# Order of the opening in an adaLN transformer kernel: third sequence's layer-norm aggregation, relu of q, and the turning of the gate columns

## The reference

```python
mod = (_silu(L0_c) @ L0_wmod).reshape(L0_c.shape[0], 6, 1, -1)
sa, ca, ga, sb, cb, gb = (mod[:, 0], mod[:, 1], mod[:, 2], mod[:, 3], mod[:, 4], mod[:, 5])
ga = (2 * (ga >= 0) - 1) * jnp.maximum(jnp.abs(ga), 0.25)      # gb alike
h = _layernorm(x, axis=-1) * (1 + ca) + sa
x = x + ga * attn_block(h)
h = _layernorm(x, axis=-1) * (1 + cb) + sb
x = x + gb * channel_mix(h)
```

## Time and profile before

| | |
|---|---|
| time, median of 3 runs | 160.79 us (160.75 to 161.41) |
| the profiled execution | 160.8 us |
| its span from first to last instruction | 159.1 us |
| granted TensorE clock | 0.999 |
| PE, PEld busy | 97%, 89% of the span |
| DVE, ACT, POOL busy | 83%, 80%, 65% |

### The profile page before, as it was taken

How to read it: one execution, slowest core, us unless ns; L and a number is a source line. 1 busy time by engine, 2 the same in 40 slices (tenths; PEclk the granted TensorE clock), 3 DMA queues, 4 the chain that set the end, 5 groups by cost and what they waited for, 6 DMA issues and landing times.

```text
span 159.1 us, 4075 instructions
## 1 busy us (share of the span) xinstructions
PE 153.6 (97%) x1127; PEld 142.4 (89%) x1127; DVE 132.2 (83%) x581; ACT 127.8 (80%) x347; POOL 104.0 (65%) x243
## 2 busy tenths in 40 slices
PE   7998999999999999999999999999999999999992
PEld 7776898989999898999999999989998999888892
DVE  3666888898998989898989899898989797887852
ACT  4455674999898989999898989898998989666562
POOL 4427667594949495867859494949587655962731
PEclk9999999999999999999999999999999999999999
DMA  4938079950010101010010101010100000010102
GB/s 127 280 116 194 12 218 339 417 220 0 2 33 4 33 0 33 6 35 0 0 37 2 33 2 37 0 35 0 37 2 24 13 29 4 0 37 4 33 15 86
DMA packets 9000, 9.95 MB, mean 63 GB/s; under 512 B 737, under 2 KB 7442, under 8 KB 8978
## 3 DMA queue, kind: packets, MB, share of 16 engines
q1 hardware_dynamic: 8656, 9.60, 19.0%
q10 hardware_dynamic: 322, 0.09, 0.2%
HBM read 7.56 MB, written 2.13 MB: 61 GB/s over the span
## 4 chain that ended last, share of the span: by engine, by line
PE 82%; DVE 5%; POOL 4%; issue 3%; ACT 2%; DMA 2%; DVEq 0%; POOLq 0%; ACTq 0%
PE bank L1161 16%; PE bank L1276 15%; PE bank L1150 8%; PE bank L1199 5%; PE bank L1232 5%; PE bank L1248 4%; PE bank L1155 4%; PE bank L1187 4%; PE bank L1240 4%; PE bank L1403 3%; PE bank L1215 3%; PE bank L1211 3%; PE bank L1259 2%; DMA x_all<-in_x 2%; POOL rstd_n L559 1%
## 5 line engine op out<-in xcount | busy, mean ns | idle before, releaser
L1276 PE MATMUL bank<-x1T,w 128*128 128x256 f32 x120 | 30.9, 381 | 0.0
L1161 PE MATMUL bank<-w,hid 128*128 128x128 f32 x240 | 30.0, 275 | 0.0
L1161 PEld LDWEIGHTS bank<-w,hid 128*128 128x128 f32 x240 | 28.5, 192 | 0.0
L559 POOL TENSOR_TENSOR rstd_n<-vare_n,power 128x2 f32<-128x2 f32 x30 | 23.5, 784 | 2.3
L552 POOL TENSOR_TENSOR vare_n<-mv_n,eps 128x2 f32<-128x2 f32 x30 | 6.1, 202 | 28.8 <-DVE mv_n L718 28.7
L354 ACT ACTIVATE hid<-bank,b_cols 128x256 f32<-128x256 f32 x60 | 23.6, 480 | 1.1 <-PE bank L1276 1.1
L1276 PEld LDWEIGHTS bank<-x1T,w 128*128 128x128 f32 x120 | 21.5, 190 | 2.5 <-ACT x1T L332 0.3
L725 DVE TENSOR_SCALAR ny<-bank,mv_ny,rstd_ny 128x128 f32<-128x128 f32 x32 | 11.7, 406 | 4.4 <-POOL rstd_ny L559 4.2
L332 ACT ACTIVATE x1T<-bank,beta_b,cols 128x256 f32<-128x256 f32 x15 | 8.5, 563 | 7.7 <-PE bank L1150 7.6
L835 DVE SCALAR_TENSOR_TENSOR mixT<-bank,modT,keepT 128x256 f32<-128x256 f32 x26 | 12.3, 475 | 1.2
L321 ACT ACTIVATE keepT<-bank,modT 128x255 f32<-128x255 f32 x26 | 13.1, 556 | 0.0
(11 more groups left out here) (183 smaller groups left out, 447.5 us busy)
## 6 DMA issues: line engine op xcount, KB each, us to landing
gm_rows<-mod_rows_dram SPq DMA_DIRECT2D x2, 960.0 KB, 10.6
out<-out_sb SPq DMA_DIRECT2D x15, 128.0 KB, 1.8
gm_rows<-mod_rows_dram SPq DMA_DIRECT2D x1, 768.0 KB, 7.1
w<-in_w SPq DMA_DIRECT2D x1, 512.0 KB, 5.4
x_all<-in_x SPq DMA_DIRECT2D x1, 512.0 KB, 5.7
bv_row<-bv_rows_dram SPq DMA_DIRECT2D x1, 512.0 KB, 7.7
bv_row<-bv_rows_dram SPq DMA_DIRECT2D x1, 384.0 KB, 4.5
gm_rows<-mod_rows_dram SPq DMA_DIRECT2D x1, 384.0 KB, 3.8
```

The costliest lines, as they stand in the source:

```text
L559: nc.gpsimd.tensor_tensor(dest[:, :], vare[name][:, :], power[:, :], ALU.pow).then_inc(rstd_ok[name], 1)
L1161: last = nc.tensor.matmul(banks[6][:, c * D:(c + 1) * D], hid[:, f, c * 128:(c + 1) * 128], w2[:, f, :], start=False, stop=(f == FF - 1 an ...
L1276: return nc.tensor.matmul(bank[:, f % 2 * L:(f % 2 + 1) * L], w1[:, f * 128:(f + 1) * 128], x1T[:, :], start=True, stop=True)
```

## The change

Four reorderings; no instruction is added or removed.

1. DVE: `x_stats(2)` stands ahead of `masked_state(0)` and `x_mv(2)` right behind it (they stood behind it, and behind `attention(0)`). On POOL `first_scale(2)` stands ahead of `gate_parts()`.
2. ACT: `q_relu()` of sequence 1 stands ahead of `state_out(1)`; that of sequence 2 stands behind `attention_turned(1)`, `x1_turned(0)` and `k_exponent(2)`.
3. PE: `attention_product(1)` stands ahead of `turn_gates()`.
4. DVE: at t = 3 `shift_of_n3(0)` stands ahead of `x_stats(5)`, `x_mv(5)` and `masked_state(3)`.

```diff
@@ ACT, first_steps
                 attention_turned(0)
+                q_relu()
                 state_out(1)
-                q_relu()
                 weights_of(2)
...
                 q_exponent(2)
-                q_relu()
                 attention_turned(1)
                 x1_turned(0)
                 k_exponent(2)
+                q_relu()
@@ POOL, first_steps
                 first_scale(1)
+                first_scale(2)
                 gate_parts()
-                first_scale(2)
                 gate_columns()
@@ DVE, first_steps
                 q_elu(0)
+                x_stats(2)
                 dve.wait_ge(const_pool, 9)
                 masked_state(0)
-
-                x_stats(2)
+                x_mv(2)
+
                 denominators(0)
                 reciprocals(0)
                 k_biased(1)
                 attention(0)
-                x_mv(2)
                 k_elu(1)
@@ DVE, step
                     norm_mv("ny", sb_ + 1)
+                    if t == 3:
+                        shift_of_n3(sp_)
                     if live(t + 2):
                         x_stats(t + 2)
                         x_mv(t + 2)
                     masked_state(sa)
-                    shift_of_n3(sp_)
+                    if t > 3:
+                        shift_of_n3(sp_)
                     y_norm(sb_)
@@ PE, first_steps
                 n1_transposes(2)
+                attention_product(1)
                 turn_gates()
-                attention_product(1)
```

## The result

| | before | after |
|---|---|---|
| time, median | 160.81 us (22 runs) | 160.34 us (22 runs) |
| ratio to before | | 0.9968, 95% interval 0.9959 to 0.9977 |
| span of the profiled execution | 159.1 us | 158.5 us |

The ratio is a gain of 0.51 us (0.37 to 0.66). The forecast was 160.55 us, a gain of 0.25 us: the time lies inside its range of 160.0 to 161.05 us, but the gain is about twice the forecast one.

A forecast was written before the change was run, and what follows sets the result against it. The prediction took TensorE, without gaps behind 16 us, to bound the kernel. From 160.8 us it took 0.28 for the opening, added 0.08 for GpSimd holding k_elu(1) and took 0.05 for the n3 shift: 160.55 us, range 160.0 to 161.05.

The forecast's parts named there:

- What bounds the kernel: Behind 16 us a row of TensorE matmuls without gaps; gains only where TensorE stands still, ahead of 16 us and in small waits.
- Part 1, aggregation: DVE and POOL, sequence 2: earlier aggregation lets n1's transposes begin near 15.18 us on TensorE, 0.65 us sooner.
- the rival (c): DVE's x_stats(2): x part 2 not landed in time, kernel slower, 161.05 us with a landing 0.5 us beyond 10.1; chance 0.04.
- Part 2: ACT's relu of q: sequence 1 brings kvs(1) to 15.45 from 16.03 us; sequence 2 taken as 0, at most 0.1 us.
- Part 3: TensorE's order: 0.4 us new wait ahead of attention_product(1); k_product(2) at 16.70 instead of 16.98 us, 0.28 of 0.65 us gained.
- Port: DVE's k_elu(1), held by GpSimd's earlier work: a loss of 0.08 us, bounds 0 and 0.28 us.
- the rival behind the term: At k_elu(1): GpSimd holds it for the full 0.28 us, leaving 160.75 to 160.8 us; chance 0.22.
- The sum: Whole kernel: 160.8 - 0.28 + 0.08 - 0.05 = 160.55 us, chance 0.58.
- Part 4: DVE's shift of n3 at t = 3: 0.05 us gained, bounds -0.1 and 0.17, most given back at state_product(4).

The follow-up runs named there:

- relu2_back: The changed kernel with relu of q of sequence 2 back ahead of attention_turned(1); ratio to before 0.9965 (0.9953 to 0.9977).
- pool_long: The changed kernel with an added SBUF-reading GpSimd sum between first_scale(2) and gate_parts; one run, attention_product(5) 39.63 us behind value_of_state(0) in its trace.
- gates_first: The changed kernel with turn_gates back ahead of attention_product(1); ratio to before 0.9958 (0.9946 to 0.9971).

## Why the prediction was right, and where it was off

- What bounds the kernel: right. Of the 0.51 us gained at the first hidden product 0.46 us are left at `attention_product(5)`. But a gain on the way isn't one at the end: the 0.09 us of the relu of sequence 2 are not among them.
- Part 1, aggregation: right in its times on DVE and TensorE. `x_stats(2)` fits in the idling ahead of `masked_state(0)`, whose place didn't move; the aggregation was forecast for 10.82 us and stands at 10.83 with the offset of 0.08, n1 for 13.85 and stands at 13.85, n1's transposes for 15.18 and stand at 15.18; the rival (c) didn't occur. The gate columns were forecast for 14.8 us and are there at 15.13, and nothing waits for them.
- Part 2: relu of sequence 1 as forecast (q_elu at 14.4 us, 0.11 us of gain through kvs). Relu of sequence 2 costed at nothing: right at the end, by relu2_back.
- Part 3: right in kind. The new wait for kvs(1) stands where it was put, at 0.35 us instead of 0.4 us. `attention_product(1)` starts at 15.75 us on the scale of before, where 15.82 was forecast, and its four instructions (two float32 matmuls) take 0.59 instead of 0.55 us: together 0.03 us better. Hence 0.31 us at `k_product(2)` where the sum had 0.28. That is in part luck: the 0.55 us was read from 16.43 to 16.98 us as the group's own pace, but it holds some 0.06 us of waiting for hT (the same group takes 0.49 us from 24.81 us on), and the group took 0.59 us because it now stands behind a wait.
- Port: **mis-sized**. The term of 0.08 us for GpSimd holding `k_elu(1)` was 0: it took 0.42 us. A gate operation was on hand (0.26 us from 12.95 us on), but ended 0.05 us behind `k_elu(1)`'s start. So `k_elu(1)` came first, and it was POOL's next operation that took longer, 0.48 instead of 0.33 us; the same happened beside `q_elu(1)` (line 594, 0.52 instead of 0.27 us), and with these 0.40 us the gate columns are late. Which of the two would come first was not worked out beforehand, and the margin was small: that the term came to nothing was luck. pool_long shows that the rival behind the term was right as a mechanism, with 0.33 us for an operation of 1.04 us, and my bound of 0.28 us was too low for an operation of that length. POOL after, and at the end the same operation before:

```profile
12.95 0.26 POOL L584 TENSOR_TENSOR gate_size<-gate_sign,raw_mod 128x32 f32<-128x32 f32 x1
13.30 0.48 POOL L586 TENSOR_SCALAR gate_pos<-gate_size 128x32 f32<-128x32 f32 x1
...
12.31 0.33 POOL L586 TENSOR_SCALAR gate_pos<-gate_size 128x32 f32<-128x32 f32 x1
```

- **The missing term: what a wait costs TensorE beyond its idling.** The sum ended at the start of `k_product(2)` and put what comes behind it at nothing. I counted the waits' ends and let the matmuls behind them run at one speed. `k_product(2)`, which waits for hT in the kernel before, takes 0.55 us from start to start (16.98 to 17.53 us) and 0.44 us after, where the gates stand ahead of it (16.59 to 17.03 us); in gates_first 0.49 us. The weight loads (PEld) of before, after and gates_first show the difference:

```profile
16.98 0.52 PEld L1232 LDWEIGHTS bank<-kqvo,hT 128*128 128x128 f32 x4
...
16.48 0.53 PEld L1235 LDWEIGHTS bank<-kqvo,hT 128*128 128x128 f32 x4
...
16.34 0.52 PEld L1235 LDWEIGHTS bank<-kqvo,hT 128*128 128x128 f32 x4
```

  Behind the wait the first load starts with the first matmul, at 16.98 us; after, it starts 0.11 us ahead, beside the matmuls of the group before; in gates_first, where hT comes just then, 0.06 us ahead. The group is shorter by just that lead. It is so again at `k_product(4)`: 0.55 us without a lead before, 0.49 us with a lead of 0.06 us after.

  Where does the gain grow from 0.31 to 0.46 us? By 0.11 us in the `k_product(2)` group, and by 0.03 us in the transposes of att (0.28 us from start to start before, 0.25 after; their loads too run ahead only after). The rest is 0.01 us net, in steps that nearly cancel: the wait for attT gives up to 0.15 us more ahead of the residual product, of which relu2_back puts 0.09 us back at the first hidden product, and by `state_product(2)` it is given back. The same lead explains part of why the swap, 0.33 us of transposes, costs only 0.16 to 0.19 us: it frees `k_product(2)` of its wait, which is worth 0.11 us against the kernel before and 0.05 us against gates_first, where the wait for att is worth 0.08 us more.
- Part 4: forecast at 0.05 us with most given back; 0.08 and 0.05 us on the way and 0 at the end.
- The sum: 0.28 - 0.08 + 0.05 = 0.25 us was forecast; 0.31 + 0 + 0 + 0.11 (group behind the wait) + 0.04 (transposes of att and the rest) = 0.46 us was measured. The forecast was low by 0.03 us for part 3, 0.08 us for the port and 0.15 us for the missing term, and high by 0.05 us for part 4.

The rest that the change has left: the order on TensorE. The prediction said that `turn_gates` would have fitted into the idling, and gates_first shows it worth 0.16 us.

## What to carry to other kernels

Where a change closes one gap, look at once for the wait that stands next in the same queue, and put work without a deadline into that one: here 0.33 us of transposes moved out of such a gap cost 0.16 of the 0.62 us that were to be had. Count a wait on TensorE as its idle time and, for 128x128 float32 weights as here, about 0.1 us more for the group behind it, whose first weights are not loaded ahead. And before a GpSimd operation is moved, see which VectorE operation with two SBUF inputs heads the chain at that time.

## What the runs showed of the hardware

A group of four matmul instructions (two float32 matmuls with 128x128 weights) on TensorE took 0.44 us when its first weight load ran 0.11 us ahead of it, 0.49 us with a lead of 0.06 us, and 0.55 us right behind a wait, in the same place of three kernels. A VectorE operation with two SBUF inputs took 0.75 instead of 0.42 us, and ended 0.28 us behind the GpSimd operation that read SBUF and was on hand when it started; beside one of nearly the same length that only wrote it took 0.43 us. When the VectorE operation came first, the GpSimd operation took longer, 0.48 instead of 0.33 us. The 0.33 us by which the reading operation held up the chain were still there 34 us further on.
